# Overlapping the quarters of a recurrence inside an attention pipeline, and moving late projections and token sums

## The reference

```
x  = L0_attn_x
xn = layernorm(x)
out = x + attn_ref(xn) + ffn_ref(xn)

attn_ref (RWKV):  h = layernorm(xn)*g1+b1;  hp = h shifted by one token
  k, v = (h*m + hp*(1-m)) @ w_tk, w_tv;   r = sigmoid((...) @ w_tr)
  y = wkv recurrence over the tokens, per channel:
      p2 = max(pp + w, w + k_t);  sum and accumulator scaled by exp(.. - p2);  pp = p2 + log(sum)
  x1 = xn + r*y;  h2 = layernorm(x1)*g2+b2, shifted and mixed into ck and cr
  out = x1 + sigmoid(cr @ w_cr) * (square(relu(ck @ w_ck)) @ w_cv)

ffn_ref (attention whose projections are low-rank mixtures of experts):
  gates from the mean of xn over the tokens (top 2 of 8 experts), per batch
  q, k, v = xn @ W_eff(gates);  16 heads of 8 channels;  softmax(q k^T) v;  @ W_eff_o
```

## Time and profile before

| | us |
|---|---|
| median of 3 runs | 485.09 (484.5 to 487.07) |
| the profiled execution | 488.56 |
| its span, first to last instruction | 486.8 |
| first places of phase A | 36.6 |
| first scores of phase B | 80.8 |
| last value product | 468.8 |

### The profile page before, as it was taken

One profiled execution on the slowest core, in us unless ns is written; L12 is line 12 of the kernel. 1 busy time (PEld: TensorE's weight loads), 2 busy tenths in 40 slices (PEclk: granted clock), 3 DMA queues, 4 the chain that ended last, 5 costly groups with the idle time before them and its releaser, 6 DMA issues.

```text
span 486.8 us, 8478 instructions
## 1 busy us (share of the span) xinstructions
PE 443.1 (91%) x3204; PEld 143.6 (29%) x3206; DVE 380.5 (78%) x678; ACT 357.3 (73%) x477; POOL 176.9 (36%) x223
## 2 busy tenths in 40 slices
PE   2988998999999999999999999999999999999993
PEld 1734323222223322222222222222222222222252
DVE  8667748899988779999887799998877999960033
ACT  3244676679988747799787477997874779979852
POOL 4032891213842332128323321283333212843300
PEclk9988998899999999999999999999999999999997
DMA  6004200213222313142223131413231302010314
GB/s 226 3 7 57 30 6 9 26 22 57 34 45 47 32 24 56 19 59 34 44 42 38 25 53 19 62 23 55 28 52 23 53 14 47 1 34 18 93 36 159
DMA packets 46332, 20.82 MB, mean 43 GB/s; under 512 B 37460, under 2 KB 37588, under 8 KB 46292
## 3 DMA queue, kind: packets, MB, share of 16 engines
q1 hardware_dynamic: 45472, 19.61, 23.8%
q10 hardware_dynamic: 820, 0.68, 0.4%
HBM read 4.88 MB, written 5.24 MB: 21 GB/s over the span
## 4 chain that ended last, share of the span: by engine, by line
PE 58%; DVE 24%; ACT 12%; DMA 2%; issue 2%; POOL 1%; SPq 0%; DVEq 0%
PE banks L1396 17%; DVE neg_half L1114 16%; PE banks L1385 13%; PE banks L1311 11%; PE banks L1357 8%; ACT probs L906 8%; DVE run L1067 3%; PE banks L1275 2%; PE banks L1208 2%; PE banks L1165 1%; ACT work L865 1%; POOL work L600 1%; DMA parts<-ctx_dram 1%; PE banks L1266 1%; ACT work L863 1%
## 5 line engine op out<-in xcount | busy, mean ns | idle before, releaser
L1114 DVE TENSOR_REDUCE neg_half<-banks 128x1 f32<-128x512 f32 x512 | 319.9, 683 | 37.5 <-PE banks L1311 36.2
L906 ACT ACTIVATE probs<-banks 128x1024 f32<-128x1024 f32 x256 | 247.8, 1022 | 63.9 <-PE banks L1385 61.2
L1396 PE MATMUL banks<-probs,v_op 128*32 128x512 f32 x1024 | 137.0, 607 | 0.4 <-ACT probs L906 0.4
L1311 PE MATMUL banks<-k_main,q_main 64*128 64x512 bf16 x512 | 121.5, 389 | 13.9 <-DVE neg_half L1114 12.2
L1385 PE MATMUL banks<-q_main,k_main 64*128 64x512 bf16 x512 | 101.1, 382 | 4.9 <-ACT probs L906 3.7
L1385 PE MATMUL banks<-q_tail,k_tail 35*128 35x512 bf16 x512 | 100.9, 381 | 0.0
L1311 PEld LDWEIGHTS banks<-k_main,q_main 64*128 64x128 bf16 x512 | 36.3, 94 | 167.5 <-DVE neg_half L1114 143.9
L1385 PEld LDWEIGHTS banks<-q_main,k_main 64*128 64x128 bf16 x512 | 26.0, 95 | 44.5 <-ACT probs L906 32.1
L1385 PEld LDWEIGHTS banks<-q_tail,k_tail 35*128 35x128 bf16 x512 | 26.6, 95 | 23.5 <-issue 0.5
L1090 DVE TENSOR_TENSOR rec<-banks,quarter_in 128x512 f32<-128x512 f32 x4 | 2.8, 692 | 37.8 <-PE banks L1357 37.8
L702 POOL TENSOR_TENSOR work<-work 128x512 f32<-128x512 f32 x12 | 12.5, 1042 | 49.7 <-ACT work L891 49.7
(11 more groups left out here) (173 smaller groups left out, 439.3 us busy)
## 6 DMA issues: line engine op xcount, KB each, us to landing
ctx_dram<-ctx_sb SPq DMA_DIRECT2D x16, 256.0 KB, 2.0
q_main<-parts SPq DMA_DIRECT2D x60, 48.0 KB
k_main<-parts SPq DMA_DIRECT2D x60, 48.0 KB
parts<-ctx_dram SPq DMA_DIRECT2D x8, 256.0 KB, 4.1
mat_sb<-in_mats_dram SPq DMA_DIRECT2D x2, 768.0 KB, 5.3
q_tail<-max_parts SPq DMA_DIRECT2D x96, 2.0 KB
v_op<-V SPq DMA_DIRECT2D x16, 64.0 KB, 3.6
out_dram<-x_sb SPq DMA_DIRECT2D x4, 256.0 KB, 3.0
```

The lines of the kernel that those rows point to most:

```text
L906: a.activation(probs[:, (2 * step + h) % 4, :, :], banks[:, 2 * h:2 * h + 2, :], ACT.Exp).then_inc(b_read, 1)
L1114: v.tensor_reduce(neg_half[:, s, u:u + 1], src, axis=AX.X, op=ALU.max, negate=True).then_inc(a_read, 1)
L1311: mm(dst, q_main[HALF * e:HALF * (e + 1), s, P * c:P * c + P], k_main[HALF * e:HALF * (e + 1), s, CHUNK * h:CHUNK * h + CHUNK], start=True ...
L1396: last = mm(banks[g:g + 32, PV_BANK, :], v_op[:, s % 2, step, e, :], probs[:, (2 * step + h) % 4, e, :], start=(step == 0), stop=(step == ...
```

## The change

- **Quarters overlap.** A quarter now takes 44 steps and one starts every 26 (`GAP`), so that for three of them the first 18 steps run beside the last 18 of the one before. Their buffers are set apart, and the carry of `h2` is taken in a step of its own. On each engine `quarters_at(step)` gives the newer quarter first, then the older. Scans are split over two steps (2 and 3, 9 and 10), the third pair stays together at 16. The order of the ring is written out as a list (`ring`) over all 128 steps.
- **Late work inside the steps.** Of the twelve mixed products six stay in the opening, and six stand in steps 2, 3, 9, 10, 15 and 16. Batch 1's projections stay in the opening, ScalarE keeps them in fp32 (`keep_late`), and GpSimd splits them in steps 2, 5, 8 and 10 (`split_late`); the eight subtractions on TensorE and the part activations of batch 1 go. GpSimd adds the bias to values 2 and 3 in steps 7 and 9.
- **Engines change.** The four clips of the weights (an activation Relu each) become `tensor_scalar` min/max on GpSimd; so do h2's scale and bias. The additions into `RT` move from VectorE to GpSimd. The copy of the transposed maxima moves from VectorE to ScalarE, after both exponentials of its step (`copy_turned`).
- **Token sums** are the accumulator of ScalarE's copy of `xnT`, done ahead of the gate; the gate's first product adds the two halves of a batch.
- The first pair's maxima of its second head are sent by ScalarE's queue, after values 3 are kept.

```diff
-FILL_JOBS.update({14 + 2 * m: [("mixed", m)] for m in range(6)})
-FILL_JOBS.update({26: [("values", 2)], 28: [("values", 3)]})
-FILL_JOBS.update({29 + (m - 6): [("mixed", m)] for m in range(6, 12)})
-FILL_JOBS.update({35 + j: [("project", j, 1)] for j in range(4)})
-FILL_JOBS.update({39 + 4 * i + j: [("part", j, 1, i)] for i in range(2) for j in range(4)})
+FILL_JOBS.update({15 + 2 * m: [("mixed", m)] for m in range(6)})
+FILL_JOBS.update({26: [("late", 0)], 28: [("late", 1)], 30: [("late", 2)], 31: [("late", 3)],
+                  38: [("values", 2)], 41: [("values", 3)]})
+LATE_MIXED = {2: 6, 3: 7, 9: 8, 10: 9, 15: 10, 16: 11}
+LATE_GATES = {12: 2, 18: 3}
+LATE_SPLITS = {2: 0, 5: 1, 8: 2, 10: 3}
+LATE_VALUES = {7: 2, 9: 3}
-PRODUCT_STEP = {"mean": 17, "var": 18, "cr": 22, "ck0": 23, "ck1": 25, "ck2": 26, "ck3": 27, "cv": 29}
+GAP = 26
+PRODUCT_STEP = {"mean": 26, "var": 28, "cr": 35, "ck0": 36, "ck1": 37, "ck2": 38, "ck3": 39, "cv": 42}
...
+        def quarters_at(step):
+            return [(step - q * GAP, q) for q in reversed(range(QUARTERS)) if step >= q * GAP]
...
+            def split_late(j):                                  # GpSimd
+                t, n = part_bank(j, 1)
+                m0, m1, m2 = (parts[:, t, i, n, :] for i in range(PARTS))
+                pool.wait_ge(late_read, j + 1)
+                g.tensor_copy(m0, late[j]).then_inc(late_part, 1)
+                pool.wait_ge(late_part, 3 * j + 1)
+                g.tensor_tensor(late[j], late[j], m0, ALU.subtract).then_inc(late_part, 1)
+                pool.wait_ge(late_part, 3 * j + 2)
+                g.tensor_copy(m1, late[j]).then_inc(late_part, 1)
+                pool.wait_ge(late_part, 3 * j + 3)
+                g.tensor_tensor(m2, late[j], m1, ALU.subtract).then_inc(late_split, 1)
...
+                if t == 13:
...
+                    clip(lo_u, -FAR, 0.0)
+                    clip(hi_u, 0.0, FAR)
+                if t == 14:
+                    clip(lo_y, -FAR, col("first"))
+                    clip(hi_y, col("first"), FAR)
...
+            def one_step(p, step):                              # GpSimd
+                now = p * KEY_TILES + step
+                for t, q in quarters_at(now):
+                    branch(t, q)
+                if now in LATE_SPLITS:
+                    split_late(LATE_SPLITS[now])
+                if now in LATE_VALUES:
+                    bias_v(LATE_VALUES[now])
+                if step == SPLIT_STEP and p + 1 < PAIRS:
+                    split_max(p + 1, (p + 1) % SETS)
...
+                a.activation(columns_of(xnT, n), bank(n), ACT.Copy, accum_out=sums[:, n:n + 1]).then_inc(xnT_ready, 1)
...
+            act.wait_ge(max_parts_ready, 1)
             for i in range(PARTS):
+                act.dma_start(q_tail[HALF + MAX_ROW + i:HALF + MAX_ROW + i + 1, 0, :],
+                              max_parts[KEY_TILES:2 * KEY_TILES, 0, i, :]).then_inc(max_in[0], 16)
...
+            def one_step(p, step):                              # ScalarE
+                now = p * KEY_TILES + step
+                exps(p, step)
+                for at in (*step_ring[now][0], *step_ring[now][1]):
+                    if is_turn(at):
+                        copy_turned(at)
+                if step == 0 and p > 0:
+                    copy_ctx(p - 1, p - 1, (p - 1) // 2)
+                for t, q in quarters_at(now):
+                    branch(t, q)
+                if now in LATE_GATES:
+                    keep_gate(LATE_GATES[now])
+                if now in LATE_MIXED:
+                    m = LATE_MIXED[now]
+                    keep_kvr(m, ring_bank(ring.index(("job", "mixed", m))))
```

More of the change, by code:

```diff
@@ L413, in program, with jobs_at @@
-        def program(eng, head, rest, tail):
-            head(0, 0, 0)
-            for p in range(PAIRS):
-                rest(p, p % SETS, p // SETS)
-                if p + 1 < PAIRS:
-                    head(p + 1, (p + 1) % SETS, (p + 1) // SETS)
-            tail()
-        def first(p):
-            return isinstance(p, int) and p == 0
+        def jobs_at(step):
+            here = [(name, q) for q in range(QUARTERS) for name, t in PRODUCT_STEP.items() if q * GAP + t == step]
+            return here + ([("mixed", LATE_MIXED[step])] if step in LATE_MIXED else [])
@@ new lines, in build @@
+        ring, step_ring = [], []
+        for n, k in places(0, A_PLACES + LEAD):
+            if exists(n, k):
+                ring.append(("place", n, k))
+        OPENING = len(ring)
+        for step in range(STEPS):
+            groups = []
+            for half in range(2):
+                ahead, unit = divmod(LEAD_UNITS + 2 * (step % KEY_TILES) + half, UNITS)
+                n = step // KEY_TILES + 1 + ahead
+                at = len(ring)
+                ring += [("place", n, k) for k in unit_places(unit) if exists(n, k)]
+                if unit == TURN_PLACE // 2 - 1 and exists(n, TURN_PLACE):
+                    ring.append(("place", n, TURN_PLACE))
+                groups.append(range(at, len(ring)))
+            at = len(ring)
+            ring += [("job", name, q) for name, q in jobs_at(step)]
+            step_ring.append((*groups, range(at, len(ring))))
@@ new lines, in ring_bank, with is_turn, filled, turned @@
+        def ring_bank(at):
+            return bank(A_BANK + at % 3)
+        def is_turn(at):
+            return ring[at][0] == "place" and ring[at][2] == TURN_PLACE
+        def filled(at):
+            return sum(kind == "place" for kind, _, _ in ring[:at + 1])
+        def turned(at):
+            return sum(is_turn(i) for i in range(at + 1))
+        def released(at):
+            kind, name, q = ring[at]
+            if is_turn(at):
+                return turn_read, turned(at)
+            if kind == "place":
+                return a_read, filled(at) - turned(at)
+            taken_by = {"mean": (centred2, q + 1), "var": (log_var_q, q + 1), "cr": (cr_step, 2 * q + 1),
+                        "cv": (gated, q + 1), "mixed": (kvr_read, q + 1)}
+            return taken_by[name] if name in taken_by else (relu_ready, q * 4 + int(name[2:]) + 1)
@@ L1447, in _ @@
-            program(pe, head, rest, tail)
+                    values(p, s, step - 1)
+                elif p > 0:
+                    values(p - 1, (p - 1) % SETS, KEY_TILES - 1)
+                for at in jobs:
+                    product(at)
+            program(one_step)
+            values(PAIRS - 1, SETS - 1, KEY_TILES - 1)
+            pe.wait_ge(b_read, PAIRS * 2 * KEY_TILES)
+            pe.wait_ge(rt_ready, QUARTERS)
+            for n in range(CHUNKS):
+                for k in range(4):
+                    mm(bank(n)[:, P * k:P * k + P], columns_of(RT, n)[:, P * k:P * k + P], ident[:, :],
+                       start=(k == 0), stop=False)
@@ L1451 @@
+            for n in range(CHUNKS):
+                pe.wait_ge(attn_ready, n + 1)
+                for k in range(4):
+                    last = mm(bank(n)[:, P * k:P * k + P], ctx_out_T[n][:, P * k:P * k + P],
+                              w_eff[:, 3, n // 2, :], start=False, stop=(k == 3))
+                last.then_inc(final_ps, 1)
 def kernel(**inputs):
```

741 lines of the change are left out of this document (334 added, 407 removed).

## The result

The changed kernel takes 462.8 us (median of 4, 461.3 to 463.8) where the kernel before took 485.8 in the same session (4 runs, 484.5 to 487.1): a ratio of 0.952, 95% interval 0.948 to 0.957. That is 23 us faster. The forecast was 470 with a range of 459 to 480; the time lies nearer to the rival "nothing waits for GpSimd" (463.5). The profiled execution took 462.16 us, span 460.4.

What follows compares the result with a forecast made beforehand. Each step lasts as long as its fullest engine, with the ring of three banks letting none run over three places ahead. The terms summed to -15.3 us: profile 473.3, median 469.8, say 470, range 459 to 480.

Steps and rivals of the forecast that it cites:

- nothing waits for GpSimd: Rival: the maxima land sooner and scans find the port free, giving 463.5 us; chance 0.27.
- The scans: Scan pairs on VectorE, split and laid under steps that TensorE products lengthen, save 11.7 us.
- The head: Token sums on ScalarE's copies bring the gate's first product from 17.1 to 14.2 and everything behind it forward: -2.9 us.
- The opening: Before the first scores: six mixed products and batch 1's subtractions go; first scores at 70.2, -7.7 us without the head.
- The maxima's path: From turned maxima through GpSimd and DMA issues to the next pair's scores: new waits of 0 to 8 us, taken as +5.
- ScalarE's full steps: Steps 12, 16, 40, 92: a weight or logarithm together with a context copy, gate or kept value costs +1.5 us.
- The weights: Clips leave ScalarE, so one weight per step fits beside the exponentials: -2.5 us over four quarters.
- RT: Two additions into RT leave VectorE in the three quarters where it still has places to read: -3.2 us.
- The late mixed products: Six mixed products on TensorE moved into the steps cost 0.86 us each, +5.2 us.
- Scan and GpSimd: VectorE scans that find GpSimd at work may wait up to 1.27 us: +1 in all, from 0 to 6.
- The clips: Clips on GpSimd take 1.1 us each; ScalarE's wait has slack for up to 2.4 us each.
- slower: Rival: clips over 2.4 us stall ScalarE, 16 us per further us; gain gone at 3.4, 494 at 3.9; chance 0.05.

Runs made afterwards that it cites:

- the shift to 27: Changed kernel with one quarter starting every 27 steps instead of every 26: 466.2 us, ratio 0.960 to the kernel before.
- The early split: Changed kernel with GpSimd's split of the maxima in step 44 put between the second and third of its five operations: 461.0 us, ratio 0.946 to the kernel before.
- the RT run: Changed kernel with the additions into RT moved back from GpSimd to VectorE: 468.4 us, ratio 0.965 to the kernel before.
- the run with five clips: Changed kernel with each of the 16 clips on GpSimd done five times over: 494.0 us, ratio 1.015 to the kernel before.

## Why the prediction was right, and where it was not

The time fell inside the range, and the mechanism was the one forecast: a step is as long as its fullest engine makes it, and scans, additions and clips cost nothing where another engine already lengthens the step or is idle. But the sum was short, -15.3 where the profiles differ by 26.4. Nearly all of its errors lie on one side: waits and costs that were added and did not come. That the total still lay in the range is owed to a lower end drawn for a case without waits, which got a chance of 0.27 and was the nearer to what happened.

*The scans, -11.7.* Right. The lone scan steps (29, 55, 81) take 3.03 to 3.04, +0.55; scans under var, cr, ck0 and cv cost nothing, and the shift to 27 gave 5.05 of the 5.1 back.

*The head, -2.9.* Right: -2.67 at the gate product, -2.6 at the scaled gates. The last accumulator read costs 0.19 us on its own, the 0.2 that was allowed for. The first places gained 3.75. The 1.15 beyond the scaled gates lies in the twelve products that copy rows for the first pair: they took 3.91 us at the lower clock before and take 2.76 now.

*The opening, -7.7: measured -10.4.* This step failed. It let ScalarE's DMA issues end the opening, after a values product it put at 66.2; that product ran at 61.13, the issues ended at 64.42, and VectorE's reads set the pace (12 in a row without a gap). The bound given "by the reads alone", 69, was still 2.3 above.

*The maxima's path, +5: measured +2.0, or +2.8 with two small waits.* The one long queue was real and where it was said to be (step 48), but 1.9 us long and not 4.1. The "0.8 in some six pairs" came in two pairs and smaller: the turned table is copied 0.6 us after the value product (201.41 against 200.82), not 2.3. Only steps 7 and 103 are longer, by 0.2 and 0.7, before the first scores of pairs 1 and 13. In step 103 the six issues end at 375.73 and the scores go at 377.00, 1.27 later, as at step 48 (210.39 and 211.53); in the profiles where the sixth issue is over 0.7 us sooner the step mostly takes 2.49. That these two are the maxima too is read from this order; no run changed it. With them the term is 2.8. The early split shows that step 47 is the split's: it returns to 2.49.

*ScalarE's full steps, +1.5: nothing.* Steps 12, 40 and 92 take 2.49; only step 16 is 0.1 above its neighbour.

*The weights, -2.5, and RT, -3.2.* Right in sign. Undoing them cost more, 4.7 and 6.5, because in the new schedule each lands on something that was not there before (the queue ahead of the split; GpSimd beside the additions) and, in the profiles, on a fall of the clock behind the stall. Seen from before, the weights' steps were 0.50 + 0.11 longer in each quarter and are plain now, 2.4 in all. The RT and cv part was 1.0 + 0.4 per quarter (7.30 to 6.30, 2.88 to 2.49), 4.2 in all.

*The turn's copy, 0.* Right; the run on VectorE gave no difference.

*The late mixed products, +5.2.* They add 1.05 to 1.19 over a plain step in steps 2, 9, 10, 15 and 16, scans included, and 0.9 in step 3 beyond its turned maxima: 6.4 in all. A little too small. The half clock, up to 74.7 us, is step 1's (3.87) and over before them.

*Scan and GpSimd, +1: about 0.7 in the scans, nothing in the steps.* The sum was nearly right and so was the rule it passed over. Timeline of the changed kernel, the late split of batch 1 and a scan of quarter 0:

```profile
97.02 0.74 DVE L1130 TENSOR_TENSOR_SCAN run<-work,run,xn_tok 128x256 f32<-128x256 f32 x1
97.09 1.08 POOL L613 CAST parts<-mat_sb 128x512 bf16<-128x512 f32 x1
...
99.47 0.61 POOL L617 CAST parts<-mat_sb 128x512 bf16<-128x512 f32 x1
100.16 1.15 POOL L619 TENSOR_TENSOR parts<-mat_sb,parts 128x512 bf16<-128x512 f32 x1
100.56 1.29 DVE L1130 TENSOR_TENSOR_SCAN run<-work,run,xn_tok 128x256 f32<-128x256 f32 x1
```

The scan that starts 0.07 us ahead of GpSimd's cast is not touched and the cast takes 1.08 instead of 0.61; the scan that starts inside GpSimd's operation takes 1.29. The 24 scans have a median of 0.74, and only two of them are over 0.8 (two to six in the other profiles). Both lie in steps that a product lengthens: step 10 takes 3.58 where step 9 takes 3.54. The additions of the RT run (2.07 for 1.05) and the scans of the run with five clips (1.74 us beside GpSimd) are the same thing. By the Trainium skill's "SBUF — State Buffer" (Who interferes with whom), whoever comes second waits whole for the shared ports; the trace agrees at these meetings. What it costs the kernel is the number of meetings that nothing hides, and here they are few; with the product moved out of step 9 one of them showed.

*The clips.* At 0.61 to 0.69 us they were shorter than the 1.1 taken, so the error in their slack stayed hidden; that was luck. It is the prediction's worst step: the rival "slower" was put at 3.4 us a clip for break-even and 3.9 for 494, and 494 came at 3.3 and 3.7, 3.5 in the mean.

The steps from the first scores to the last value product fell by 12.2 where the terms said 4.7. The terms' errors: 2.2 for the maxima, 1.5 for ScalarE, 1.0 for the port, 1.0 for cv and RT, 0.5 for the scans, less 0.9 for the mixed products, 5.3 together. What had no term: the mean steps (3.87 to 3.66, 0.9 in all) and the step ahead of cr (2.62 to 2.49, 0.4). The first value product comes 0.7 sooner behind the scores, but step 1 takes 3.87 instead of 3.08, so these two cancel. The last 12 steps are 3.5 shorter (32.97 to 29.45); three of the last quarter's products now lie ahead of them and cost 2.3 there (steps 113 to 115), so 1.2 is gained. That is 7.8 for the 7.5 to be explained. None of the four items without a term was separated by a run.

## What to carry to other kernels

Place work of one engine in the very steps that another engine lengthens, and count only those steps: the slack of a neighbouring step was worth nothing here, where a ring of three banks ties the engines. Before giving an operation to an idle engine, list what stands behind it in that engine's queue and who waits for each of those, since the slack belongs to the last of them and not to the operation's own reader. And price an undone edit in the new schedule, not in the old: the same additions, with the cv step around them, cost 1.4 us a quarter before and 1.8 or more after.

## What the hardware showed that was not expected

The granted clock of TensorE, at 1.2 GHz or 2.4 GHz, follows small gaps. In the changed kernel TensorE is busy 4.51 of the 6 us from 62 to 68 (gaps of 0.21 us between places), and then the clock is 0.50 from 68 to 74 in that profile and in its repeat; with the gaps filled it stays at 1.00, in both kernels that fill them. In five of the eight profiles whose opening was left as it is up to there, the clock was already 0.72 to 0.84 somewhere between 56 and 68 us with the same work, and the first value product came 0.6 to 1.9 us later than in the changed kernel's profile. So executions of the same work differ by that much through the clock; what starts the earlier fall is open. The head has such a spread too: with the same head the clock rises at 13.5 to 14.5 us in four profiles, whose first places stand at 30.9 to 31.3, and at 18.4 to 20.1 in eight, where they stand at 32.3 to 32.9. And a stall of TensorE has a second price that comes only sometimes: of nine stalls of 1.5 to 1.9 us in the steps (the five-fold clips left out) two were followed by 3.4 us at half clock, at 1.55 and 1.6 us; the longer one of 2.42 us was as well. The same stall before step 48 has it in one profile and not in five others. A price read from one profile can thus hold a clock's fall that the next execution doesn't have.

On ScalarE the accumulator's output is an instruction of its own behind the activation (0.19 us each). On GpSimd a clip with two bounds, 128x512 fp32, takes 0.61 us with two constants and 0.69 with one bound from a column, against 1.03 to 1.29 for an operation with two tensors.
